# Zeros selected by GpSimd in the exponentials in place of mask products in the second score pass, with the scatters cut into groups around it

## The chip, the cores and the metric

The kernel runs on one core of a Trainium2 chip. The metric is the device time of one execution in microseconds; the lower, the better. Engines are named as the profile does: PE is TensorE (PEld its weight loads), DVE is VectorE, ACT is ScalarE, POOL is GpSimd, SP is SyncE.

## The reference

Sixteen sequences of 512 tokens with 256 features go through layer norm, causal attention with 16 heads of 16, and a mixture of 32 experts of which each token takes four, beside a shared expert:

```python
scores = jnp.einsum('bqhd,bkhd->bhqk', q, k) * scale
causal = jnp.triu(jnp.ones((S, S), dtype=bool), k=1)
scores = jnp.where(causal, -jnp.inf, scores)
attn = jax.nn.softmax(scores, axis=-1)
out = jnp.einsum('bhqk,bkhd->bqhd', attn, v)
...
x = x + _L0_attn_ref(xn, ...) + _L0_ffn_ref(xn, ...)
```

What matters here is the causal mask: a key later than the query must have weight zero.

## The kernel before

The program has three stretches. Phase A goes through the 16 sequences ("batches" below), one after another: attention, the shared expert, and the routing of each token to its four experts. Phase B and C take the 288 blocks of routed tokens through their experts, phase D adds up. Each phase is a block of its own: the next begins when all engines have come to the end of the one before.

In phase A all engines run one list of steps, `ORDER`, and each engine does what its handler for a step says (`run`). So the list sets the order on every engine. The steps of the next sequence's front part (layer norm, q and k products, value and router products) are mixed into the attention of the current one; the last sequence has no next one, and these steps are left out of its list (`attention_steps`). Batch 0 stands ahead of the loop, batches 1 to 14 are the loop, batch 15 is the `tail`.

The heads are done in four groups g of four heads. For each group:

- `("s1", g, u)`, six units: scores with queries on the partitions, for the row maximum. PE multiplies q by k (L937) and adds the mask by a product of the identity with `mask_qk` (L941); DVE takes the maximum (L729). `negsplit` and `negT` (L741, L951) turn the maxima into two extra rows of q, which a DMA puts in place (L409).
- `("s2", g, u)`, five units: scores with keys on the partitions, now less the maximum (L968). PE then adds `mask_kq`, -1e30 above the diagonal, by products with the identity (L979), two a unit. Units 0 and 1 have one diagonal square of 128 columns per head pair, units 2 to 4 have two. ACT writes the exponential of the unit to `probs[g % 2]` (L598). `probs[0]` lies in the space of `we_d`, by which name the trace shows it; `probs[1]` is `probs`.
- `("av", g, kt)`, four steps: the exponentials times the values (L996), kt being the tile of 128 keys. Before, the first of them waits for all five units of the group.

s1 and s2 units share two PSUM buffers (`ps_u`) in turn, so a unit can start when the unit two before it has been read by DVE or ACT.

POOL has two kinds of work in phase A. For `("qk", j)`, j from 0 to 3, it adds the two rope products of DVE (L479), waits until ACT has made the first part (`part0`, L544), and subtracts (L483). For `("scat", t)` it issues for each of the 16 pairs of token tile and expert choice two indirect DMAs, one to `table` (L492) and one to `values` (L494). ACT's `copy` step and DVE's `rankC` of the next batch wait until all of a batch's scatters have landed. In the last batch a step `fill` follows the last scatter: 32 indirect DMAs of zeros (L500). POOL waits for all of them at the end of phase A.

Of the kernel before, what the change touches and what calls it, by code (L numbers as in the profile page):

```python
# [26 lines left out]
BF16 = mybir.dt.bfloat16  # L27
# [7 lines left out]
P = 128  # L35
# [18 lines left out]
REGION = TOKENS  # L54
NBLOCK = TOKENS * TOPK // P + E
TABLE = E * REGION + P
N_CONSTS, N_EARLY, N_IDENT = 24, 22, 4
SKIP = 1 << 24
EPS = 1e-5
MAGIC = float(0x5F3759DF)  # L60
# [8 lines left out]
def hold(eng, passed):  # L69
# [7 lines left out]

ORDER = [
    ("rankC",), ("gate", 0), ("placeV",), ("s1", 0, 0), ("gth", 0), ("up", 0), ("s1", 0, 1), ("copy",), ("s1", 0, 2),
    ("gate", 1), ("s1", 0, 3), ("s1", 0, 4), ("gth", 1), ("scat", 0), ("up", 1), ("lnA",), ("gate", 2), ("s1", 0, 5),  # L80
    ("negsplit", 0), ("gth", 2), ("scat", 1), ("s1", 1, 0), ("up", 2), ("s1", 1, 1), ("negT", 0), ("gate", 3),
# [11 lines left out]
    ("exps",), ("stack", 1), ("down", 0), ("down", 1), ("rankA",), ("av", 3, 0), ("av", 3, 1), ("av", 3, 2),  # L93
    ("av", 3, 3), ("rankB",), ("down", 2), ("avT", 3), ("down", 3), ("aT", 0), ("aT", 1), ("oproj", 0), ("oproj", 1),
]

# [5 lines left out]
def last_steps(order):  # L102


    s, piece = [], 0
    for step in order:
        s.append(step)
        if step == ("rankC",):
            s.append(("fill_rows",))
        if step == ("scat", NT - 1):  # L110
            s.append(("fill",))
        if step[0] == "s2" and step[1:] != (0, 0) and piece < GU_PIECES:
            s.append(("load_gu", piece))
            piece += 1
        if step == ("s2", NG - 1, NU2 - 1):
            s += [("load_d", k) for k in range(D_PIECES)]
    assert piece == GU_PIECES
    return s
# [75 lines left out]
def phase_a(nc, sb_, sem, ident, identb, iota_e, counts, we_gu, we_d, ps_g, ps_u, ps_av, x, wqkvr, wgu_e, wd_e, wo, wgu_s, wd_s, bias,  # L194
            rope_cos, rope_sin, values, sum_dram, table):
    stack = ExitStack()
    with stack:
# [28 lines left out]
        sin_t = in_gu([P, SEQ])  # L226
        ident_r = sb("ident_r", [P, P], F32R)
        mask_qk = sb("mask_qk", [P, P], BF16)
        mask_kq = sb("mask_kq", [P, P], BF16)
        before = sb("before", [P, P], BF16)  # L230
        ones = sb("ones", [P, P], BF16)
        tri_f = sb("tri_f", [P, P])
# [70 lines left out]
        xn_ready, parts_ready, v_placed = sem("xn_ready"), sem("parts_ready"), sem("v_placed")  # L303
        v_ready = sem("v_ready")
        summed, part0_ready = sem("summed"), sem("part0_ready")
        passed_pool, passed_dve, passed_sp = sem("passed_pool"), sem("passed_dve"), sem("passed_sp")
        we_in, fill_chain, fill_ready, filled = sem("we_in"), sem("fill_chain"), sem("fill_ready"), sem("filled")
        neg_parts, tanh_done, av_out, exps, chosen_ready = \
# [119 lines left out]
        def _(pool):  # L428
# [33 lines left out]
                            allow_small_or_imprecise_dtypes=True))  # L462
            zeros_kept(NEG, 0, 1, -1)
            const(pool.tensor_copy(mask_qk[:], tri_f[:]))
            zeros_kept(NEG, 0, -1, 1)
            const(pool.tensor_copy(mask_kq[:], tri_f[:]))
            zeros_kept(1.0, 0, 1, -1)
            const(pool.tensor_copy(before[:], tri_f[:]))
            assert made[0] == N_EARLY
# [14 lines left out]
                                   ALU.subtract).then_inc(parts_ready, 1)  # L484

            def scatter(b, step, env):
                t = step[1]
                pool.wait_ge(xs_ready, NT * b + NT)
                pool.wait_ge(slots, b + 1)
                hold(pool, passed_pool)  # L490
                for k in range(TOPK * t, TOPK * (t + 1)):
                    pool.indirect_dma_start(table[:, :], bass.IndirectOffsetOnAxis(ap=slot[:, k:k + 1], axis=0),  # L492
                                            entry[:, k, :], None).then_inc(scattered, 16)
                    pool.indirect_dma_start(values[:, :], bass.IndirectOffsetOnAxis(ap=slot[:, k:k + 1], axis=0),  # L494
                                            xs[:, k // TOPK, :], None).then_inc(scattered, 16)

            def fill(b, step, env):
                pool.wait_ge(fill_ready, 1)
# [10 lines left out]

                    pool.wait_ge(table_set, 16)  # L510

            run(pool, {"loaded": loaded, "qk": qkv, "scat": scatter, "fill": fill})
            pool.wait_ge(filled, 16 * E)
            pool.wait_ge(scattered, SCATTERS * BATCH)

# [347 lines left out]
        def _(pe_):  # L863
# [92 lines left out]
            def s2(b, step, env):  # L956

                _, g, u = step
                ps = unit_of(step, env)
                if isinstance(b, int) and (b, g, u) == (0, 0, 0):  # L960
                    pe_.wait_ge(consts, N_CONSTS)
                if u == 0:
                    pe_.wait_ge(neg_rows[g % 2], 32 * (2 * b + g // 2 + 1))
                for lo, kt, k in S2_PIECES[u]:
                    n, h = SEQ - kt * P, 2 * g + k
                    for a in range(2):
                        rows = slice(HALF * a, HALF * a + MROWS)
                        nc.tensor.matmul(ps[:, a, lo:lo + n], k_st[rows, h, kt * P:(kt + 1) * P],  # L968
                                         q_st[rows, h, kt * P:SEQ], start=(lo == 0), stop=False, skip_group_check=True)
                for a in range(2):  # L970
                    if u < 2:
                        dst, rhs = ps[:, a, 0:P], mask_kq[:]
                    else:
                        if u < 4:
                            dst = ps[:, a, :].rearrange("p (k n) -> p k n", n=P)[:, 0:NT:3, :]
                        else:
                            dst = ps[:, a, :].rearrange("p (k n) -> p k n", n=2 * P)[:, :, 0:P]
                        rhs = mask_kq[:].rearrange("p (o n) -> p o n", o=1).broadcast_to([P, 2, P])
                    ins = nc.tensor.matmul(dst, identb[:], rhs, start=False, stop=True, skip_group_check=True)  # L979
                ins.then_inc(pe["s2"], 1)  # L980

            def av_(b, step, env):

                _, g, kt = step
                if kt == 0:
                    pe_.wait_ge(S["probs"], done("probs", b, NU2 * g + NU2 - 1))
                    pe_.wait_ge(av_out, NG * b + g)
                    if g == 0:
                        pe_.wait_ge(v_placed, b + 1)
# [489 lines left out]
```

## Time and profile before

| | before |
|---|---|
| median of 3 runs | 2126.34 us (2124.21 to 2130.44) |
| profiled execution, its own time | 2123.62 us |
| its span | 2121.8 us |
| granted PE clock, mean | 0.93 |
| PE busy | 1841.0 us, 87% |
| DVE busy | 1313.1 us, 62% |
| POOL busy | 995.3 us, 47% |
| ACT busy | 812.4 us, 38% |

Phase A takes the first 1475 us or so, phases B and C run to about 2095, phase D takes the rest. A busy share is one over all of the span; what bounds phase A is read from the rows further down.

### The profile page before, as it was taken

To read this page: it belongs to the slowest core of one execution; us is meant where nothing else is said; L and a number is where in the kernel's file an instruction comes from. 1 tells how busy PE (TensorE), PEld (TensorE's weight loads), DVE (VectorE), ACT (ScalarE), POOL (GpSimd) and SP (SyncE) were. 2 spreads that over 40 slices of the span, in tenths; PEclk is the share of its full clock that TensorE was granted. 3 is DMA by queue.
4 is the path that set the end of the run, shared out by engine and by line. 5 is a ranking of instruction groups with operands and counts; after the bars stand their busy time and mean duration, and the time that the engine had idled before them with its cause. 6 is when DMAs were issued, how large, how long until landed. Compare 5 with 4: busy or idle time off the path is not lost. (4 is left out here: it accounts for less than half of the span.)

```text
span 2121.8 us, 42143 instructions
## 1 busy us (share of the span) xinstructions
PE 1841.0 (87%) x10799; PEld 1131.5 (53%) x10800; DVE 1313.1 (62%) x3315; ACT 812.4 (38%) x1763; POOL 995.3 (47%) x993
## 2 busy tenths in 40 slices
PE   5899999999999999999999999996899999999400
PEld 2354554545545455454554545543688888888300
DVE  6656648576585665856648566551566666666487
ACT  2334344353443434435344353432344444445200
POOL 4455344453444534545444453465455565555200
PEclk8999999999999999999999999987899999999755
DMA  6251541615416154161441615466465555555399
GB/s 134 77 123 35 104 79 52 119 37 104 76 55 118 35 106 79 52 122 38 100 80 51 120 37 102 71 169 229 131 176 170 169 175 171 169 165 175 129 351 324
DMA packets 217708, 255.02 MB, mean 120 GB/s; under 512 B 74421, under 2 KB 166334, under 8 KB 217536
## 3 DMA queue, kind: packets, MB, share of 16 engines
q1 hardware_dynamic: 160000, 161.90, 34.2%
q0 software_dynamic: 35840, 71.63, 10.5%
q10 hardware_dynamic: 21824, 20.98, 3.1%
q8 instruction: 19, 0.31, 0.1%
q14 instruction: 25, 0.20, 0.0%
HBM read 112.54 MB, written 94.64 MB: 98 GB/s over the span
## 5 line engine op out<-in xcount | busy, mean ns | idle before, releaser
L729 DVE TENSOR_REDUCE neg<-ps_u 128x2 f32<-128x768 f32 (+3 forms) x384 | 391.6, 1044 | 161.6 <-PE ps_u L941 157.4
L492 POOL DMA_INDIRECT table<-entry,slot x256 | 248.9, 972 | 390.2 <-ACT xs L576 291.7
L1228 POOL DMA_INDIRECT y_dram<-yb,ent x288 | 283.0, 983 | 225.1 <-issue 168.2
L494 POOL DMA_INDIRECT values<-xs,slot x256 | 252.3, 985 | 83.4 <-issue 83.4
L921 PE MATMUL ps_g<-we_gu 128*128 128x512 f32 x512 | 243.7, 609 | 0.0
L937 PE MATMUL ps_u<-k_st,q_st 48*128 48x128 f32 (+3 forms) x1024 | 184.2, 397 | 31.4 <-DVE neg L729 20.3
L598 ACT ACTIVATE probs<-ps_u 128x1024 f32<-128x1024 f32 x160 | 159.6, 1023 | 128.2 <-PE ps_u L979 128.1
L598 ACT ACTIVATE we_d<-ps_u 128x1024 f32<-128x1024 f32 x160 | 160.6, 1022 | 116.9 <-PE ps_u L979 116.9
L968 PE MATMUL ps_u<-q_st,k_st 50*128 50x512 f32 (+3 forms) x1024 | 170.9, 393 | 39.0 <-DMA q_st<-neg_t 16.6
L479 POOL TENSOR_TENSOR we_d<-we_d 128x512 f32<-128x512 f32 x64 | 81.1, 1268 | 216.7 <-DVE we_d L699 216.7
L937 PEld LDWEIGHTS ps_u<-k_st,q_st 48*128 48x128 f32 x1024 | 87.3, 187 | 166.3 <-issue 76.0
L1279 PE MATMUL ps_u<-we_d,h_t 128*128 x576 | 173.8, 384 | 0.0
L1265 PE MATMUL ps_g<-we_gu,x_t 128*128 x576 | 150.8, 385 | 4.4 <-issue 4.4
L968 PEld LDWEIGHTS ps_u<-q_st,k_st 50*128 50x128 f32 x1024 | 88.3, 199 | 122.4 <-ACT probs L598 32.4
L1360 DVE TENSOR_SCALAR wh<-ent 128x1 f32<-128x1 f32 x288 | 44.4, 154 | 176.4 <-ACT tnh L1175 137.5
L1265 PE MATMUL ps_av<-we_gu,x_t 128*128 x576 | 150.1, 383 | 1.6 <-issue 1.5
L1026 PE MATMUL ps_u<-w_d,hid 128*128 128x256 f32 x512 | 135.4, 418 | 0.6
L921 PEld LDWEIGHTS ps_g<-we_gu 128*128 128x128 f32 x512 | 92.8, 194 | 80.2 <-issue 75.5
L1353 DVE COPY x_t<-ps_g 128x256 f32<-128x256 f32 x288 | 120.5, 418 | 12.1 <-PE ps_g L1254 10.5
L941 PE MATMUL ps_u<-mask_qk,identb 128*128 128x128 bf16 (+1 forms) x768 | 125.0, 245 | 0.0
L1189 ACT ACTIVATE yb<-ps_u 128x256 f32<-128x256 f32 x288 | 110.6, 384 | 31.3 <-PE ps_u L1279 5.2
L902 PE MATMUL ps_g<-we_gu 128*128 128x512 f32 x256 | 121.2, 596 | 0.0
(161 smaller groups left out, 3005.4 us busy)
## 6 DMA issues: line engine op xcount, KB each, us to landing
xg<-values SPq DMA_DIRECT2D x288, 128.0 KB
ys<-y_dram SPq DMA_DIRECT2D x64, 512.0 KB, 5.4
q_st<-we_gu SPq DMA_DIRECT2D x192, 128.0 KB, 8.6
k_st<-we_gu SPq DMA_DIRECT2D x192, 128.0 KB, 10.4
we_gu<-x SPq DMA_DIRECT2D x16, 512.0 KB, 5.2
xres<-x SPq DMA_DIRECT2D x16, 512.0 KB, 4.5
sum_dram<-osum SPq DMA_DIRECT2D x16, 512.0 KB, 3.7
we_gu<-wgu_e ACTq DMA_DIRECT2D x16, 512.0 KB, 5.1
```

Of the source, the lines that this page charges most:

```text
L492: pool.indirect_dma_start(table[:, :], bass.IndirectOffsetOnAxis(ap=slot[:, k:k + 1], axis=0), entry[:, k, :], None).then_inc(scattered, 16)
L494: pool.indirect_dma_start(values[:, :], bass.IndirectOffsetOnAxis(ap=slot[:, k:k + 1], axis=0), xs[:, k // TOPK, :], None).then_inc(scatte ...
L598: nc.scalar.activation(probs[g % 2][:, u, :], ps_u[env[1][step][0]][:, :, :].rearrange("p a n -> p (a n)"), ACT.Exp, scale=SCALE).then_inc ...
L729: nc.vector.tensor_reduce(neg[:, g % 2, i, :, k0:k0 + nk], ps[:, :, 0:nk * n].rearrange("p a (k n) -> p a k n", n=n), AX.X, ALU.max, negat ...
L921: ins = nc.tensor.matmul(ps[:, :], w_gu[:, c, lo:lo + P], xn_t[:, c, :], start=(c == 0), stop=(c == KC - 1))
L937: nc.tensor.matmul(ps[:, a, k * n:(k + 1) * n], q_st[rows, h, i * P:(i + 1) * P], k_st[rows, h, 0:n], start=(k == 0), stop=False, skip_gro ...
L941: ins = nc.tensor.matmul(dst, identb[:], mask_qk[:].rearrange("p (o n) -> p o n", o=1).broadcast_to([P, nk, P]), start=False, stop=True, s ...
L968: nc.tensor.matmul(ps[:, a, lo:lo + n], k_st[rows, h, kt * P:(kt + 1) * P], q_st[rows, h, kt * P:SEQ], start=(lo == 0), stop=False, skip_g ...
L1026: nc.tensor.matmul(ps[:, t // 2, (t % 2) * D:(t % 2 + 1) * D], hid[:, m, t * P:(t + 1) * P], w_d[:, m, :], start=(t % 2 == 0 and m == 0), ...
L1228: pool.indirect_dma_start(y_dram[:, :], bass.IndirectOffsetOnAxis(ap=ent[k][:, 0:1], axis=0), yb[k][:, :], None, bounds_check=TOKENS * TOP ...
L1265: ins = nc.tensor.matmul(ps_gu[s][:, 0:2 * HE], x_t[s][:, c * P:(c + 1) * P], w_gu[:, bass.ds(e, 1), c, :], start=(c == 0), stop=(c == KC ...
L1279: nc.tensor.matmul(ps_y[s][:, 0:D], h_t[s][:], w_d[:, bass.ds(e, 1), :], start=True, stop=True).then_inc(y_ps, 1)
```

## The change

`mask_kq` and the 40 products a batch that add it are gone; each score product of s2 is now a group by itself (`start=True, stop=True`). A new step `("zero", g, i)` lets POOL write zeros above the diagonal into the exponentials, in place: i = 0 after units 0 and 1 (one instruction of 4 squares), i = 1 after units 2 and 3 (two instructions), i = 2 after unit 4 (one). Each handles 512 columns on 128 partitions. The first three `av` steps of a group wait for one `zero` step each, the first no longer for all exponentials. `("scat", t)` becomes `("scat", first, end)` in pairs: 8, 2, 2, 1, 1 and 2 of them, at other places in the list, the last two pairs behind `("zero", 3, 2)`. `fill` stays behind the last scatter.

```diff
@@ ORDER (cut)
-    ("gate", 1), ("s1", 0, 3), ("s1", 0, 4), ("gth", 1), ("scat", 0), ("up", 1), ("lnA",), ("gate", 2), ("s1", 0, 5),
+    ("gate", 1), ("s1", 0, 3), ("s1", 0, 4), ("gth", 1), ("scat", 0, 8), ("up", 1), ("lnA",), ("gate", 2), ("s1", 0, 5),
...
@@ last_steps
-        if step == ("scat", NT - 1):
+        if step[0] == "scat" and step[2] == NT * TOPK:
             s.append(("fill",))
@@ gpsimd
+            def zero(b, step, env):
+
+                _, g, i = step
+                u0, nu, step_, cnt = [(0, 2, SEQ, 1), (2, 2, 3 * P, 2), (4, 1, 2 * P, 2)][i]
+                pool.wait_ge(S["probs"], done("probs", b, NU2 * g + u0 + nu - 1))
+                hold(pool, passed_pool)
+                at = probs[g % 2][:, u0:u0 + nu, :].rearrange("p u n -> p (u n)")
+                if cnt == 2 and step_ == 2 * P:
+                    views = [at.rearrange("p (w n) -> p w n", n=2 * P)[:, :, 0:P]]
+                else:
+                    views = [at.rearrange("p (w n) -> p w n", n=SEQ)[:, :, lo:lo + P] for lo in range(0, SEQ, 3 * P)[:cnt]]
+                for view in views:
+                    ins = pool.affine_select(out=view, in_=view, compare_op=ALU.is_ge, fill=0.0, base=0,
+                                             pattern=[[0, 4 if nu > 1 or step_ == 2 * P else 2], [1, P]], channel_multiplier=-1)
+                ins.then_inc(zeroed, 1)
@@ tensor, s2
-                        nc.tensor.matmul(ps[:, a, lo:lo + n], k_st[rows, h, kt * P:(kt + 1) * P],
-                                         q_st[rows, h, kt * P:SEQ], start=(lo == 0), stop=False, skip_group_check=True)
...
-                    ins = nc.tensor.matmul(dst, identb[:], rhs, start=False, stop=True, skip_group_check=True)
+                        ins = nc.tensor.matmul(ps[:, a, lo:lo + n], k_st[rows, h, kt * P:(kt + 1) * P],
+                                               q_st[rows, h, kt * P:SEQ], start=True, stop=True, skip_group_check=True)
@@ tensor, av
+                if kt < 3:
+                    pe_.wait_ge(zeroed, 3 * (NG * b + g) + kt + 1)
                 if kt == 0:
-                    pe_.wait_ge(S["probs"], done("probs", b, NU2 * g + NU2 - 1))
                     pe_.wait_ge(av_out, NG * b + g)
```

Two places on POOL and one on PE show what the list now does. First POOL in the loop, from the subtract of `("qk", 1)` on, around `("qk", 2)`, `("qk", 3)` and group 1 of the heads. Before:

```order
L479 TENSOR_TENSOR we_d<-we_d 128x512 [waits rope,parts_ready]
L483 TENSOR_TENSOR we_gu<-we_d,we_gu 128x512 [waits part0_ready,stacked1]
L475 REGISTER_ALU
L479 TENSOR_TENSOR we_d<-we_d 128x512 [waits rope,parts_ready]
L483 TENSOR_TENSOR we_gu<-we_d,we_gu 128x512 [waits part0_ready,stacked1]
L492 DMA table<-entry,slot 262272x2 [waits xs_ready,slots]
```

The same place in the changed kernel:

```order
L478 TENSOR_TENSOR we_d<-we_d 128x512 [waits rope,parts_ready]
L482 TENSOR_TENSOR we_gu<-we_d,we_gu 128x512 [waits part0_ready,stacked1]
L499 REGISTER_ALU
L507 AFFINE_SELECT probs1<-probs1 128x4x128 [waits probs]
L499 REGISTER_ALU
L507 AFFINE_SELECT probs1<-probs1 128x4x128 [waits probs]
L507 AFFINE_SELECT probs1<-probs1 128x4x128
L474 REGISTER_ALU
L478 TENSOR_TENSOR we_d<-we_d 128x512 [waits rope,parts_ready]
L482 TENSOR_TENSOR we_gu<-we_d,we_gu 128x512 [waits part0_ready,stacked1]
L499 REGISTER_ALU
L507 AFFINE_SELECT probs1<-probs1 128x4x128 [waits probs]
```

Three selects now stand between the subtract of `("qk", 2)` and the add of `("qk", 3)`, and the fourth, `("zero", 1, 2)`, stands behind the subtract of `("qk", 3)`.

PE at `("av", 1, 0)` to `("av", 1, 3)`, in the changed kernel:

```order
L1001 MATMUL ps_av<-probs1,v_pad 32x512 [waits av_out,zeroed]
L1001 MATMUL ps_av<-probs1,v_pad 32x512 x3
L990 REGISTER_ALU
L1001 MATMUL ps_av<-probs1,v_pad 32x384 [waits zeroed]
L1001 MATMUL ps_av<-probs1,v_pad 32x384 x3
L990 REGISTER_ALU
L1001 MATMUL ps_av<-probs1,v_pad 32x256 [waits zeroed]
L1001 MATMUL ps_av<-probs1,v_pad 32x256 x3
L1001 MATMUL ps_av<-probs1,v_pad 32x128 x4
```

Before, only the first of these rows had a wait (`av_out,probs`); now the third key tile waits for the select that stands behind `("qk", 3)` on POOL.

Last, POOL at the end of the last batch, in the changed kernel, from `("zero", 3, 0)` to the end of phase A:

```order
L507 AFFINE_SELECT probs1<-probs1 128x4x128 [waits probs] x2
L507 AFFINE_SELECT probs1<-probs1 128x4x128
L507 AFFINE_SELECT probs1<-probs1 128x4x128 [waits probs]
L490 DMA table<-entry,slot 262272x2 [waits xs_ready,slots]
L492 DMA values<-xs,slot 262144x256
L490 DMA table<-entry,slot 262272x2
L492 DMA values<-xs,slot 262144x256
L514 DMA values<-zeros,fill_row 262144x256 [waits fill_ready]
L514 DMA values<-zeros,fill_row 262144x256 x31
L198 UNCONDITIONAL_BRANCH [waits scattered,filled]
```

Before, the 32 scatters of the batch and the 32 fills followed each other with no wait for `probs` among them; now the last four scatters and all 32 fills stand behind the last exponential of the last batch.

## Rows read from the trace of the kernel before

**Rows 1.** Busy time of each engine in a stretch of one batch (--windows)
```profile
core 0: us, PE busy (x) PEld busy (x) DVE busy (x) ACT busy (x) POOL busy (x), PEclk, DMA share, GB/s
853.90:942.50 88.60, 83.67 (x512) 45.83 (x512) 56.68 (x122) 35.30 (x57) 41.22 (x41) 0.96 0.40 79
```

**Rows 2.** Waits of PE, 300 to 1500 us: total, times, longest
```profile
PE ps_u L968 <- DMA q_st<-neg_t: 14.6, 14, 2.2
PE ps_g L951 <- DVE neg_p L741: 13.3, 14, 1.1
```

**Rows 3.** Timeline of PE, one batch: start us, us, idle before
```profile
714.46 0.28 PE L979 MATMUL ps_u<-mask_kq,identb 128*128 128x128 bf16 x2
714.67 0.50 PE L968 MATMUL ps_u<-q_st,k_st 50*128 50x384 f32 x4
...
715.86 0.50 PE L968 MATMUL ps_u<-q_st,k_st 50*128 50x384 f32 x4 [0.36 <-ACT probs L598]
716.29 0.39 PE L979 MATMUL ps_u<-mask_kq,identb 128*128 128x256 bf16 x2
716.52 1.88 PE L902 MATMUL ps_g<-we_gu 128*128 128x512 f32 x4
...
721.80 2.36 PE L996 MATMUL ps_av<-probs,v_pad 128*32 128x512 f32 x32
724.09 0.44 PE L937 MATMUL ps_u<-k_st,q_st 48*128 48x384 f32 x2
```

**Rows 4.** Timeline of ACT in the same batch
```profile
714.78 2.96 ACT L598 ACTIVATE probs<-ps_u 128x1024 f32<-128x1024 f32 x3 [4.44 <-PE ps_u L979]
717.76 0.63 ACT L544 ACTIVATE we_gu<-we_d 128x512 fp32r<-128x512 f32 x1
...
741.14 4.91 ACT L598 ACTIVATE probs<-ps_u 128x1024 f32<-128x1024 f32 x5 [1.16 <-PE ps_u L979]
```

**Rows 5.** Timeline of POOL in the same batch
```profile
718.54 1.28 POOL L483 TENSOR_TENSOR we_gu<-we_d,we_gu 128x512 fp32r<-128x512 f32 x1 [0.81 <-ACT we_gu L544]
720.77 1.27 POOL L479 TENSOR_TENSOR we_d<-we_d 128x512 f32<-128x512 f32 x1 [0.96 <-DVE we_d L699]
722.85 1.28 POOL L483 TENSOR_TENSOR we_gu<-we_d,we_gu 128x512 fp32r<-128x512 f32 x1 [0.81 <-ACT we_gu L544]
```

**Rows 6.** POOL's groups by form: the selects that there are (mean ns)
```profile
L442 POOL TENSOR_SCALAR_AFFINE_SELECT tri_f<-tri_f 128x128 f32<-128x128 f32 x3 | 0.9, 292 | 0.4
...
L1222 POOL TENSOR_SCALAR_AFFINE_SELECT tri<-tri 32x32 f32<-32x32 f32 x1 | 0.2, 202 | 0.1
```

**Rows 7.** Timeline of POOL at the end of phase A
```profile
1424.60 0.97 POOL L494 DMA_INDIRECT values<-xs,slot  x1 [0.30 <-issue]
1425.87 1.00 POOL L500 DMA_INDIRECT values<-zeros,fill_row  x1 [0.31 <-issue]
...
1465.86 0.98 POOL L500 DMA_INDIRECT values<-zeros,fill_row  x1 [0.30 <-issue]
1478.84 0.37 POOL L1216 IOTA blk_i<- 32x288 f32 x1 [12.00 <-POOLq L197]
```

**Rows 8.** Timeline of ACT at the end of phase A
```profile
1449.38 3.98 ACT L598 ACTIVATE probs<-ps_u 128x1024 f32<-128x1024 f32 x4
```

**Rows 9.** Timeline of SP at the end of phase A
```profile
1468.97 0.40 SPq L415 DMA_DIRECT2D sum_dram<-osum  x1
```

**Rows 10.** Landing times: line L415, and the page's DMA issues (KB, us)
```profile
DMA to landing us min/median/max: 3.1/3.7/5.9
```
```profile
y_dram<-yb,ent POOLq DMA_INDIRECT x288, 2.7
```

**Rows 11.** One step of three batches, timeline of PE
```profile
756.30 0.92 PE L1035 MATMUL ps_u<-w_o,attn_t 128*128 128x256 f32 x3 [0.25 <-ACT attn_t L613]
...
842.55 0.70 PE L1035 MATMUL ps_u<-w_o,attn_t 128*128 128x256 f32 x2 [0.25 <-ACT attn_t L613]
...
931.43 1.35 PE L1035 MATMUL ps_u<-w_o,attn_t 128*128 128x256 f32 x5 [0.25 <-ACT attn_t L613]
```

**Rows 12.** Granted clock (PEclk) of one stretch, columns as in Rows 1
```profile
727.00:735.00 8.00, 7.72 (x36) 4.29 (x34) 2.43 (x5) 3.54 (x5) 6.17 (x7) 0.57 0.19 62
```

More of the change, by code:

```diff
@@ L56 @@
 TABLE = E * REGION + P
-N_CONSTS, N_EARLY, N_IDENT = 24, 22, 4
+N_CONSTS, N_EARLY, N_IDENT = 21, 19, 4
 SKIP = 1 << 24
@@ L79 @@
     ("rankC",), ("gate", 0), ("placeV",), ("s1", 0, 0), ("gth", 0), ("up", 0), ("s1", 0, 1), ("copy",), ("s1", 0, 2),
-    ("gate", 1), ("s1", 0, 3), ("s1", 0, 4), ("gth", 1), ("scat", 0), ("up", 1), ("lnA",), ("gate", 2), ("s1", 0, 5),
-    ("negsplit", 0), ("gth", 2), ("scat", 1), ("s1", 1, 0), ("up", 2), ("s1", 1, 1), ("negT", 0), ("gate", 3),
[11 rows of a table removed]
-    ("exps",), ("stack", 1), ("down", 0), ("down", 1), ("rankA",), ("av", 3, 0), ("av", 3, 1), ("av", 3, 2),
+    ("gate", 1), ("s1", 0, 3), ("s1", 0, 4), ("gth", 1), ("scat", 0, 8), ("up", 1), ("lnA",), ("gate", 2), ("s1", 0, 5),
+    ("negsplit", 0), ("gth", 2), ("s1", 1, 0), ("up", 2), ("s1", 1, 1), ("negT", 0), ("gate", 3),
[6 rows of a table added]
+    ("s2", 1, 4), ("zero", 1, 2), ("negT", 2),
[5 rows of a table added]
+    ("zero", 3, 1), ("rank",), ("s2", 3, 4), ("zero", 3, 2), ("scat", 14, 16), ("exps",), ("stack", 1), ("down", 0), ("down", 1), ("rankA",), ("av", 3, 0), ("av", 3, 1), ("av", 3, 2),
     ("av", 3, 3), ("rankB",), ("down", 2), ("avT", 3), ("down", 3), ("aT", 0), ("aT", 1), ("oproj", 0), ("oproj", 1),
@@ L228, in phase_a @@
         mask_qk = sb("mask_qk", [P, P], BF16)
-        mask_kq = sb("mask_kq", [P, P], BF16)
         before = sb("before", [P, P], BF16)
@@ L305, in phase_a @@
         summed, part0_ready = sem("summed"), sem("part0_ready")
+        zeroed = sem("zeroed")
         passed_pool, passed_dve, passed_sp = sem("passed_pool"), sem("passed_dve"), sem("passed_sp")
@@ L464, in _ @@
             const(pool.tensor_copy(mask_qk[:], tri_f[:]))
-            zeros_kept(NEG, 0, -1, 1)
-            const(pool.tensor_copy(mask_kq[:], tri_f[:]))
             zeros_kept(1.0, 0, 1, -1)
@@ L486, in scatter @@
             def scatter(b, step, env):
-                t = step[1]
                 pool.wait_ge(xs_ready, NT * b + NT)
@@ L490, in scatter @@
                 hold(pool, passed_pool)
-                for k in range(TOPK * t, TOPK * (t + 1)):
+                for k in range(step[1], step[2]):
                     pool.indirect_dma_start(table[:, :], bass.IndirectOffsetOnAxis(ap=slot[:, k:k + 1], axis=0),
@@ L510, in loaded @@
                     pool.wait_ge(table_set, 16)
-            run(pool, {"loaded": loaded, "qk": qkv, "scat": scatter, "fill": fill})
+            run(pool, {"loaded": loaded, "qk": qkv, "scat": scatter, "zero": zero, "fill": fill})
             pool.wait_ge(filled, 16 * E)
@@ L967, in s2 @@
                         rows = slice(HALF * a, HALF * a + MROWS)
-                        nc.tensor.matmul(ps[:, a, lo:lo + n], k_st[rows, h, kt * P:(kt + 1) * P],
-                                         q_st[rows, h, kt * P:SEQ], start=(lo == 0), stop=False, skip_group_check=True)
[L970 to L978, printed above, removed]
-                    ins = nc.tensor.matmul(dst, identb[:], rhs, start=False, stop=True, skip_group_check=True)
+                        ins = nc.tensor.matmul(ps[:, a, lo:lo + n], k_st[rows, h, kt * P:(kt + 1) * P],
+                                               q_st[rows, h, kt * P:SEQ], start=True, stop=True, skip_group_check=True)
                 ins.then_inc(pe["s2"], 1)
```

20 rows, old and new, of the table ORDER are left out of this document.

## The prediction

> **What bounds the kernel now.** I read first the busy time of each engine in a stretch of one batch. In 88.6 us PE is busy 83.67, DVE 56.68, POOL 41.22 and ACT 35.30 [rows 1]. So PE sets the pace of phase A, and what shortens its queue shortens the batch, unless something else is then late. Next I read PE's waits. They are short and belong to chains: over thirteen batches 14.6 us for the DMA of the maxima and 13.3 us for the DVE step ahead of `negT` [rows 2]. The reader is to see that work removed just ahead of such a wait only lengthens the wait. Third comes the timeline of one batch on PE, ACT and POOL, since the change adds a wait of PE on POOL, and POOL works in the order of the list. Last comes the end of phase A, where POOL's last DMAs are issued until 1466.84 [rows 7] and SP's last store is issued at 1468.97 [rows 9]: two ends that lie close together, so either can become the later one.
>
> **What the removal gives.** A pair of mask products takes 714.67 - 714.46 = 0.21 us of PE's time with one square and 716.52 - 716.29 = 0.23 us with two [rows 3]. (Their listed durations, 0.28 and 0.39, overlap the work behind them; the distance to the next start is what goes away.) A batch has 8 of the first and 12 of the second, 4.4 us. Not all of it comes back. ACT needs some 0.99 us for a unit (2.96 for three, 4.91 for five [rows 4]), and PE may be only two units ahead, so in a run of s2 units only the first unit's mask moves the chain of exponentials. By group:
> - group 0: units 0, 3, 4 count, 1 and 2 don't: 0.21 + 0.23 + 0.23 = 0.67.
> - group 1: unit 2 doesn't (the unit behind it waits 0.36 for ACT already [rows 3]): 0.21 + 0.21 + 0.23 + 0.23 = 0.88.
> - group 2: unit 0 is ahead of an s1 unit that waits for DVE, unit 4 ahead of `negT` that waits for DVE [rows 2]; units 1, 2, 3 count. Units 2 and 3 fall in a stretch whose granted clock is 0.57 in the mean [rows 12], so mostly at 1.2 GHz and not 2.4, and count double: 0.21 + 0.46 + 0.46 = 1.13.
> - group 3: five exponentials in one run [rows 4]: only the first mask and the last, 0.44.
>
> Together 3.12 us a batch.
>
> **What a select costs.** The trace has selects of 128 columns (292 ns) and of 32 columns (202 ns) [rows 6]. That is 0.94 ns a column, and 292 + 384 x 0.94 = 653 ns for 512 columns. The bounds: no less than the 292 ns of a select of a quarter of the size, and no more than the 1.27 us of the POOL instruction with two inputs of 512 columns [rows 5]. I take 0.65, because the same operation is in the trace and only its length differs. Sixteen a batch are 10.4 us, and POOL goes from 41.2 to about 52 of 88.6 us busy. It doesn't become the bound; the question is where its work lies.
>
> The page "GPSIMD Engine Reference" of the Trainium skill speaks against the move: its table in section 4.1 gives elementwise work to VectorE, and section 3.1 has 769 ns as measured for 512 elements with one input. By that figure, as an estimate, the four selects in the chain of the next part would take 4 x 0.12 = 0.5 us more a batch, and the sum would be 7 us higher.
>
> **What the order costs PE.** In group 1, POOL's subtract of `("qk", 2)` ends at 718.54 + 1.28 = 719.82 [rows 5]. It follows ACT's part0, which follows the third exponential of the run [rows 4], and this run starts 0.2 earlier now: 719.6. Then come `("zero", 1, 0)` with one select and `("zero", 1, 1)` with two; with 0.1 us ahead of the first they take from 719.7 to 721.7. The add of `("qk", 3)`, before at 720.77 [rows 5], starts at 721.75 and ends at 723.0; ACT's part lies between add and subtract as before (0.81 us of idle [rows 5]); the subtract ends at 725.1, and `("zero", 1, 2)` at 725.9. PE can go on with the third key tile at 726.0.
>
> Where would PE be? Before, av(1) runs from 721.80 to 724.09 [rows 3]. Less the masks of units 1, 3 and 4 of this group it starts at about 721.15; the four key tiles have 512, 384, 256 and 128 columns, so the third starts at 70% of the 2.29 us, at 722.75. PE stands idle for 726.0 - 722.75 = 3.25 us, in each of the 15 batches that have qk steps. Behind it in PE's queue are the s1 and s2 units of groups 3 and 2, and so DVE and ACT wait too: nothing makes up for it. The bounds by the price of a select (four of them lie in this chain): 3.25 - 4 x 0.36 = 1.8 us and 3.25 + 4 x 0.62 = 5.7 us.
>
> At the other av steps I find no wait. In group 0 the 16 scatters are done before the exponentials matter; in group 2 the select behind one scatter pair (2.5 us) ends about when the third key tile comes, and PE waits for a DMA right behind it anyway [rows 2]; in group 3 the down products lie between. The last scatters of a batch stand behind the last exponentials now; what hides them is the end of the batch on PE (av, down and output products) ahead of the next `rankC`, and if they landed behind that, DVE and then PE would wait there.
>
> Per batch: 3.25 - 3.12 = +0.13 us, over 15 batches +2 us. The whole gain on PE goes into the wait.
>
> **What the order costs at the end of phase A.** In the last batch POOL ran from scatter to fill with no wait; the fills took 1465.86 - 1425.87 = 39.99 us for 31 starts, 1.29 each, and the last ended at 1466.84 [rows 7]. Now four scatters and 32 fills stand behind `("zero", 3, 2)`, and that behind the last exponential, which ended at 1449.38 + 3.98 = 1453.36 [rows 8]. The masks ahead of it in this batch give at most 2.9; more of its units queue on ACT and DVE, and I take 2.3: 1451.1. Then 0.1 + 0.65 for the select, 4 x 1.27 = 5.1 for the scatters (spacing 1425.87 - 1424.60 [rows 7]), 32 x 1.29 = 41.3 for the fills: the last ends at 1498.2. Landing: 2.7 us from issue as the scatters of phase B have it [rows 10], so 1499.9. Before, the last store was issued at 1468.97 [rows 9] and lands 3.7 later [rows 10], at 1472.7; POOL's first instruction of phase B came at 1478.84 [rows 7], 6.1 later. Now it comes at 1506.0: +27.2 us. Nothing covers it, since phase B starts behind the barrier.
>
> **Sum.** 2 + 27.2 = +29 us, from a span of 2121.8 to about 2151. The profiled execution's own time is 2123.62, 1.8 over its span and 2.7 under the median of the runs; against the median 2126.34 I forecast **2155.5 us**, 1.4% slower. About 0.3% (6 us) is what a measurement of this kernel can tell from no change.
>
> **Rivals.**
> - *More time at the low clock.* Most batches have one stretch at 1.2 GHz such as [rows 12]. The batch that ends at 842.55 has none and took 86.25, the one after took 88.88 [rows 11]: one stretch costs 2.6 us. The clock falls in group 2, after a few waits of 0.3 to 0.4 us. Now a wait of 3 us comes just ahead, and the dense products of the masks are gone. If a second stretch follows in each batch: 15 x 2.6 = +39, 2195 us. Against it: the fall may only come where it comes already. Chance 0.22. The page "TensorE: Matmul & The Clock Gate", Part 1, says that the throttled state is the default and activity releases it; that would speak for this rival, and by it alone I would raise its chance.
> - *A select costs as much as a two-input instruction*, 1.27 us: the wait is 5.7, so +37 more, 2192 us. For it: 3-dimensional views with strides, which the rows do not show. Chance 0.11.
> - *av(1) is not late* (the other side): POOL's selects would fit ahead of PE. Then the 3.12 us come back in full: -47 + 27 = -20, 2107 us, faster. It decides from the point where the wait at the third key tile is under 3.12 - 27.2 / 15 = 1.3 us; that is below my lower bound of 1.8. For it: POOL's listed spans are rough, and a PE that keeps more of the 4.4 us moves the point. Chance 0.14.
> - *The low stretch goes away* because the order of waits changes: at most in 14 of the 15 batches, -36, with the two costs as forecast: 2119 us, at the edge of 0.3%. Chance 0.08.
> - *The mask gain is whole*, 4.4 us and not 3.1, with the rest as forecast: -19, 2136 us. Part of the range of the forecast.
>
> **How the numbers follow.** Forecast 0.45; its own range is 2136 (the mask gain whole) to 2174 (a select of 0.96 us, half way to its upper bound: 15 x 4 x 0.31 = +19). The others 0.22, 0.11, 0.14, 0.08. The range leaves out the fast rival and a little above: 2118 to 2198. Faster: 0.14 and 0.03 of the last rival but one, 0.17. Same: the rest of that rival's 0.08 and a little of the forecast's lower edge, 0.08. Slower: 0.75.
>
> **What would show it.** The rows of the mask products are gone and s2 units lie 0.2 us closer. A select of 128x4x128 shows 0.65 us. PE's waits have a new row, av on POOL, about 3 us in 15 batches, in one step of group 1. POOL's fills run from about 1459 to 1500 and phase B starts some 27 us later. Wrong would be: no such wait (POOL in time), a select of over 1 us, a batch with two stretches of low clock, or PE waiting for `rankC` because the late scatters land late.

## The result, and the profile after

The changed kernel takes 2213.02 us in the median (2207.28 to 2217.81, 4 runs) against 2125.28 us before: a ratio of 1.042, 95% interval 1.0383 to 1.0457. It is 88 us slower, three times the 29 us that I forecast, and above the range. The span grew from 2121.8 to 2211.8 us, the mean granted clock fell from 0.930 to 0.886.

The waits of PE in the changed kernel, over the whole span: who waited for whom, us in total, times, longest:

```profile
PE ps_av L1001 <- POOL probs L507: 40.0, 15, 3.0
PE ps_u L982 <- ACT probs L612: 24.4, 49, 0.9
PE ps_g L965 <- DVE neg_p L755: 23.6, 31, 1.4
```

The first row is new, and it is the wait that was forecast: 15 times, 2.67 us each (forecast 3.25). (L507 is the select, L982 the s2 product, L965 `negT`.) The two below it are larger than before (ACT `probs` 5.9, `neg_p` 16.5 us over phase A): PE's units are shorter by their masks, the ACT and DVE steps that they wait for are not.

Where the wait sits is read from the timelines of one batch. PE:

```profile
1116.38 0.74 PE L982 MATMUL ps_u<-q_st,k_st 50*128 50x512 f32 x6
1118.01 0.50 PE L982 MATMUL ps_u<-q_st,k_st 50*128 50x384 f32 x4 [0.88 <-ACT probs L612]
...
1123.60 1.71 PE L1001 MATMUL ps_av<-probs,v_pad 128*32 128x512 f32 x16
1127.91 0.86 PE L1001 MATMUL ps_av<-probs,v_pad 128*32 128x256 f32 x16 [2.60 <-POOL probs L507]
```

and POOL in the same batch:

```profile
1120.91 1.27 POOL L482 TENSOR_TENSOR we_gu<-we_d,we_gu 128x512 fp32r<-128x512 f32 x1 [0.81 <-ACT we_gu L558]
1122.13 1.81 POOL L507 TENSOR_SCALAR_AFFINE_SELECT probs<-probs 128x512 f32<-128x512 f32 x3
1123.91 1.28 POOL L478 TENSOR_TENSOR we_d<-we_d 128x512 f32<-128x512 f32 x1
1126.00 1.26 POOL L482 TENSOR_TENSOR we_gu<-we_d,we_gu 128x512 fp32r<-128x512 f32 x1 [0.81 <-ACT we_gu L558]
1127.22 0.64 POOL L507 TENSOR_SCALAR_AFFINE_SELECT probs<-probs 128x512 f32<-128x512 f32 x1
```

This is the queue of the prediction: subtract, three selects, add, 0.81 us for ACT, subtract, and only then the select for which the third key tile waits. The wait at L982 has gone from 0.36 us [rows 3] to 0.88: a mask taken out in the middle of a run of exponentials.

What I had left to a rival is in the granted clock. The columns are those of [rows 1]; the first fence is the middle of phase A before, the second the same stretch after, with the two stretches that follow the wait shown above:

```profile
600.00:1300.00 700.00, 659.64 (x4067) 359.03 (x4067) 448.05 (x961) 283.95 (x447) 327.33 (x316) 0.97 0.40 78
```
```profile
600.00:1300.00 700.00, 633.67 (x3581) 336.96 (x3572) 435.10 (x928) 263.69 (x423) 385.94 (x420) 0.91 0.37 76
...
1124.00:1128.00 4.00, 1.40 (x20) 0.35 (x16) 0.93 (x1) 0.63 (x1) 3.04 (x3) 1.00 0.01 2
1129.00:1147.00 18.00, 16.57 (x84) 7.96 (x82) 9.26 (x27) 7.65 (x11) 9.60 (x11) 0.53 0.21 54
1149.00:1154.00 5.00, 4.52 (x23) 3.58 (x22) 1.78 (x8) 2.34 (x4) 3.35 (x6) 0.66 1.09 132
```

The clock is at 2.4 GHz while PE stands, falls to 1.2 GHz within 2 us of PE going on at 1127.91, and stays there for most of 18 us; a short second stretch follows. In windows of 1 us all 15 batches with the wait show this fall right behind it; the stretch is 17 or 18 us long in eight of them and 11 in the other seven. Before, a stretch in the middle batches was 7 or 8 us long [rows 12]. As a measure of the low clock I add up, over phase A until PE's last product, stretch length times one minus the granted clock ("clock loss", worked out from windows of 1 us): 61 us before, 150 us after. It is read from one execution of each kernel; `e4_fill_spread` below, whose batches 0 to 14 are those of the changed kernel, shows 164, so differences of 15 us or less say nothing.

The end of phase A, POOL:

```profile
1515.69 0.98 POOL L490 DMA_INDIRECT table<-entry,slot  x1 [0.16 <-issue]
...
1520.80 1.00 POOL L514 DMA_INDIRECT values<-zeros,fill_row  x1 [0.31 <-issue]
...
1560.83 0.98 POOL L514 DMA_INDIRECT values<-zeros,fill_row  x1 [0.30 <-issue]
1571.27 0.37 POOL L1221 IOTA blk_i<- 32x288 f32 x1 [9.45 <-POOLq L198]
```

and ACT there, whose last exponential ends at 1514.46:

```profile
1513.41 1.05 ACT L612 ACTIVATE probs<-ps_u 128x1024 f32<-128x1024 f32 x1
```

From the end of the last exponential to POOL's first instruction of phase B it is 56.8 us now, 25.5 before (1478.84 - 1453.36, [rows 7, 8]): 31.3 us for the late fill. Phase B begins 92.4 us later; so the late fill has 31 us of it and the batches 61, of which 40 are PE standing for POOL. (Of the 31, 6.3 us are the last select and four scatters, which stand between the exponential and the first fill: 1520.80 - 1514.46.)

### The profile page after: what moved, and what is told of

Read it like the earlier page. It is cut to its first block and busy times, and to the rows that moved or that the text cites. A ratio compares the mean times of both kernels' runs of the same rounds, so it can differ in the third digit from the quotient of the medians.

```text
span 2211.8 us, 41662 instructions
## 1 busy us (share of the span) xinstructions
PE 1833.7 (83%) x10159; PEld 1116.1 (50%) x10160; DVE 1315.4 (59%) x3315; ACT 806.6 (36%) x1763; POOL 1152.3 (52%) x1246
## 5 line engine op out<-in xcount | busy, mean ns | idle before, releaser
L935 PE MATMUL ps_g<-we_gu 128*128 128x512 f32 x512 | 243.3, 608 | 0.0
L951 PE MATMUL ps_u<-k_st,q_st 48*128 48x128 f32 (+3 forms) x1024 | 198.1, 425 | 36.9 <-DVE neg L743 21.4
L982 PE MATMUL ps_u<-q_st,k_st 50*128 50x512 f32 (+3 forms) x1024 | 168.0, 410 | 48.1 <-ACT probs L612 24.4
L612 ACT ACTIVATE probs<-ps_u 128x1024 f32<-128x1024 f32 x160 | 153.5, 1030 | 86.8 <-PE ps_u L982 84.5
L951 PEld LDWEIGHTS ps_u<-k_st,q_st 48*128 48x128 f32 x1024 | 92.9, 198 | 181.6 <-issue 72.7
L982 PEld LDWEIGHTS ps_u<-q_st,k_st 50*128 50x128 f32 x1024 | 93.2, 216 | 130.7 <-ACT probs L612 49.2
L955 PE MATMUL ps_u<-mask_qk,identb 128*128 128x128 bf16 (+1 forms) x768 | 131.0, 256 | 0.0
L916 PE MATMUL ps_g<-we_gu 128*128 128x512 f32 x256 | 127.4, 621 | 0.0
```

The lines of the kernel that those rows point to most:

```text
L612: nc.scalar.activation(probs[g % 2][:, u, :], ps_u[env[1][step][0]][:, :, :].rearrange("p a n -> p (a n)"), ACT.Exp, scale=SCALE).then_inc ...
L935: ins = nc.tensor.matmul(ps[:, :], w_gu[:, c, lo:lo + P], xn_t[:, c, :], start=(c == 0), stop=(c == KC - 1))
L951: nc.tensor.matmul(ps[:, a, k * n:(k + 1) * n], q_st[rows, h, i * P:(i + 1) * P], k_st[rows, h, 0:n], start=(k == 0), stop=False, skip_gro ...
L955: ins = nc.tensor.matmul(dst, identb[:], mask_qk[:].rearrange("p (o n) -> p o n", o=1).broadcast_to([P, nk, P]), start=False, stop=True, s ...
L982: ins = nc.tensor.matmul(ps[:, a, lo:lo + n], k_st[rows, h, kt * P:(kt + 1) * P], q_st[rows, h, kt * P:SEQ], start=True, stop=True, skip_g ...
```

## The experiments

Two theories of the batches' 61 us were put against each other. **Wait theory**: PE's wait for POOL brings the extra low clock. **Thin-work theory**: the clock falls because the dense mask products are gone. Each ratio is to the kernel before on the same chip; differences between two variants that ran on different chips carry the 3 us by which the kernel before differs there (2123.10 to 2126.31).

**Masks out, nothing else** (`e1_no_masks`; nothing above the diagonal is zeroed).

```diff
-  q_st[rows, h, kt * P:SEQ], start=(lo == 0), stop=False, skip_group_check=True)
-  ... # the loop over a that adds mask_kq
+  q_st[rows, h, kt * P:SEQ], start=True, stop=True, skip_group_check=True)
```


> The kernel before with the mask products of s2 taken out and nothing in their place: no selects, scatters and fill where they were, PE waits for the exponentials as before. What lies above the diagonal is not zeroed, so this leaves out half of the causal mask. Wait theory (the extra time at 1.2 GHz in the changed kernel comes from PE's wait for POOL): no such wait here, the clock stays about as before (mean some 0.93) and the time falls by the 3.1 us a batch that I worked out: about 2075 us. Thin-work theory (the clock falls because the dense bf16 products are gone): the stretches at the low clock grow as in the changed kernel, by about 4 us a batch, and the time is 2125 - 50 + 60 = about 2135 us with a mean clock near 0.89.

Measured: 2095.73 us, ratio 0.9865 (0.9834 to 0.9895), 30.6 us faster; clock loss 68 us, not to be told from 61. The clock stays, against the thin-work theory taken alone. But the gain is 1.9 us a batch, not 3.1. PE's waits in one batch give the place:

```profile
858.89 0.50 PE L968 MATMUL ps_u<-q_st,k_st 50*128 50x384 f32 x4 [0.88 <-ACT we_d L598]
859.81 0.44 PE L937 MATMUL ps_u<-k_st,q_st 48*128 48x384 f32 x2 [0.41 <-ACT we_d L598]
...
882.35 0.50 PE L968 MATMUL ps_u<-q_st,k_st 50*128 50x384 f32 x4 [0.88 <-ACT probs L598]
...
899.61 0.59 PE L951 MATMUL ps_g<-ident_r,neg_p 128*8 128x128 f32 x4 [1.60 <-DVE neg_p L741]
...
908.20 3.72 PE L1016 MATMUL ps_u<-w_d,hid 128*128 128x256 f32 x16 [0.41 <-ACT probs L598]
```

Before, the waits there were 0.46, none, 0.36, 1.08 and none. Over that batch all waits of PE sum to 7.2 us against 4.65 in the batch before the change that ends at 842.55: 2.6 of the 4.4 us of masks come back as waits, where I had counted 1.3. The last row is one I had counted as saved: the down products take over a score buffer and wait for ACT's run of five.

**Masks kept, all else changed** (`e2_masks_kept`): the mask products are back on PE beside the selects.

```diff
+  ... # the loop over a that adds mask_kq, as before the change
```


> The changed kernel with the mask products of s2 put back on PE, so that the selects write zeros where there are zeros already. The wait for POOL and the late fill stay. Wait theory: the low clock stays as in the changed kernel and the masks add up to 3.1 us a batch: 2213 + 50 = about 2260 us. Thin-work theory: the low clock goes back to that of before (about 4 us a batch less): 2213 + 50 - 60 = about 2200 us.

Measured: 2200.71 us, ratio 1.0346 (1.0322 to 1.0371); PE waits 31.5 us for POOL, clock loss 92 us. With the masks the kernel is faster than without them: 12 us less, though PE has 640 products more. So a wait with the masks in place costs more than its length (clock loss 61 to 92), and with the masks out it costs more still (150). The two waits are not quite the same: 2.1 us a batch here, 2.67 in the changed kernel. With the masks the clock falls behind the wait in 11 of the 15 batches, without them in all.

**The third and fourth key tile later on PE** (`e3_av_later`); `avT` of the group moves one unit back with them.

```diff
-  ("av", 1, 0), ("av", 1, 1), ("av", 1, 2), ("av", 1, 3), ("scat", 10, 12), ("s1", 3, 2), ("s2", 2, 0), ("s1", 3, 3),
-  ("s1", 3, 4), ("s2", 2, 1), ("zero", 2, 0), ("avT", 1), ("s2", 2, 2),
+  ("av", 1, 0), ("av", 1, 1), ("scat", 10, 12), ("s1", 3, 2), ("s2", 2, 0), ("s1", 3, 3), ("s1", 3, 4),
+  ("av", 1, 2), ("av", 1, 3), ("s2", 2, 1), ("zero", 2, 0), ("s2", 2, 2), ("avT", 1),
```


> The changed kernel with the third and fourth key tile of group 1 four steps later on PE (behind the s1 and s2 units that followed them), so that POOL's select is done when PE comes to them. Masks stay out, the fill stays late. Wait theory: 2.7 us of wait and about 4 us of low clock a batch go away, 15 x 6.7 = 100: about 2113 us, the clock at about 0.93. Thin-work theory: the wait alone goes: 2213 - 40 = about 2173 us, the clock stays near 0.89.

Measured: 2142.26 us, ratio 1.0074 (1.0048 to 1.0101), 71 us off; clock loss 90 us. The wait's 40 us and 30 more go. The measured time lies between the two forecasts.

**The select between POOL's add and subtract**, where POOL waits 0.81 us anyway. PE's order is untouched. It ran twice: first on a chip on which the kernel before took 2641.82 us (told at the end), then on another.

```diff
   pool.tensor_tensor(rq[:, j % 2, :], rp1[:, j % 2, :], rp2[:, j % 2, :], ALU.add).then_inc(summed, 1)
...
+  if j == 3 and not env[3]:
+      zero(env[2], ("zero", 1, 2), env)
   pool.wait_ge(part0_ready, NCH * nb + j + 1)
```


> The changed kernel with the last select of group 1 put between POOL's add and subtract for the q/k step 3, where POOL waits for ACT anyway; PE's order is that of the changed kernel. The wait at the third key tile shrinks from 2.7 to about 0.7 us: 15 x 2 = -30 us from that alone, 2183 us (thin-work theory, clock still near 0.89). Wait theory: nearly all the extra low clock goes too, 60 us more, about 2125 us. If both are needed together (what the masks kept and the later av steps suggest): in between, near the later av steps, 2145 to 2160 us with Sum of low clock near 90 us in phase A.

> The same kernel once more on another chip: the changed kernel with the last select of group 1 between POOL's add and subtract for q/k step 3. Thin-work theory: only the wait shrinks, 2183 us. Wait theory: the wait and nearly all extra low clock, 2125 us. Both needed: 2145 to 2160 us.

Measured on the second chip: 2147.36 us, ratio 1.011 (1.0069 to 1.015). PE's waits in phase A:

```profile
PE ps_u L988 <- ACT probs L618: 24.1, 49, 0.9
...
PE ps_av L1007 <- POOL probs L509: 8.7, 15, 1.0
```

31 us of wait gone, 66 us of time gone, clock loss from 150 to 94 us. It is the cleanest pair: one instruction moved on an engine that is not the bottleneck. Over half of what it saves is clock: PE's busy time in phase A, with the same products, falls from 1320.8 to 1277.2 us (rows further down). Neither theory alone forecasts it (2183 and 2125); "both together" does (2145 to 2160).

**The late fill.** In the kernel before, the fills alone wait for the last exponential:

```diff
   def fill(b, step, env):
+      pool.wait_ge(S["probs"], done("probs", b, NG * NU2 - 1))
       pool.wait_ge(fill_ready, 1)
```


> The kernel before, with one wait added on POOL in the last batch: the 32 fills wait for the last exponential. Nothing else is touched; all scatters are issued before. My account of the end of phase A: fills from about 1453.5 to 1494.8, landing and barrier as forecast: phase B starts some 24 us later, 2126 + 24 = about 2150 us. If the end of phase A is set otherwise: 2126 us, no change.

> The same kernel once more on another chip, since on the first one both kernels took some 500 us more than elsewhere: the kernel before with the 32 fills of the last batch waiting for the last exponential. Late fill as I account for it: +24 us, 2126 to 2150. Otherwise: no change.

Measured on the second chip: 2147.03 us, ratio 1.0113 (1.0074 to 1.0151), +23.3 us; on the first 0.9946 (0.9926 to 0.9966): there the late fill cost nothing that can be seen, against the forecast, and why is not known. POOL in the second chip's trace:

```profile
1451.85 0.99 POOL L501 DMA_INDIRECT values<-zeros,fill_row  x1 [27.26 <-ACT probs L599]
...
1502.26 0.37 POOL L1217 IOTA blk_i<- 32x288 f32 x1 [9.44 <-POOLq L197]
```

Phase B starts 23.4 us later than before, as worked out. The other way round, the fills cut up in the changed kernel (`e4_fill_spread`):

```diff
+FILL_AT = {("scat", 8, 10): (0, 6), ("zero", 1, 0): (6, 7), ("scat", 10, 12): (7, 12), ("zero", 2, 0): (12, 13),
+           ("scat", 13, 14): (13, 16), ("scat", 14, 16): (16, 32)}
```


> The changed kernel with the 32 fills of the last batch in six pieces, 16 of them in POOL's idle time between selects and scatters, 16 behind the last scatter. My account of the end of phase A (+27 us forecast for the late fill, +31 by the two traces): 16 x 1.29 = 20.6 us come off, 2192 us. If instead the end of phase A is set by something else (the weight loads or the last output product), it stays within 5 us of 2213.

Measured: 2199.57 us, ratio 1.035 (1.0328 to 1.0372), 13.4 us off instead of 20.6. In the traces the end of phase A is shorter by the full amount and more: from PE's last product to phase B it is 20.2 us instead of 42.7. But PE's last product ends 9 us later. Some 6 us of this were there before the last batch, in batches that the edit does not touch (its clock loss is 164 against 150). In the last batch the fills in POOL's "idle" time made a select late, and PE with it:

```profile
1513.99 1.51 PE L1003 MATMUL ps_av<-we_d,v_pad 128*32 128x256 f32 x16 [1.58 <-POOL we_d L509]
```

**The selects on a scratch tile** (`e8`, `f8`): POOL waits for the exponentials and selects as in the change, but on other data and with a wait of 0.17 us between one select and the next, and PE waits for the exponentials alone. Nothing above the diagonal is zeroed; the last batch has POOL's waits but no selects.

```diff
+  view = aside[:, 0, :].rearrange("p (w n) -> p w n", n=P)
...
-  pe_.wait_ge(zeroed, 3 * (NG * b + g) + kt + 1)
+  pe_.wait_ge(S["probs"], done("probs", b, NU2 * g + NU2 - 1))
```


> The changed kernel with the selects of batches 0 to 14 working on a scratch tile instead of the exponentials (those of the last batch are left out, its waits on POOL stay), and PE waiting for the exponentials as before. So nothing above the diagonal is zeroed; masks are out, POOL has its selects, the scatters and the late fill are where the change put them. If POOL's work costs the others nothing: e1 (2096) + late fill (31) = about 2127 us, low clock as in e1. If POOL's selects or the moved scatters slow other engines or make DVE wait: up to 2143 us, as with the later av steps.

> The same kernel once more on another chip: selects on a scratch tile (none in the last batch), PE waits for the exponentials as before, masks out, scatters and late fill as in the change; nothing above the diagonal is zeroed. POOL's work costs the others nothing: 2127 us. It slows them or lowers the clock: up to 2143 us.

Measured on the second chip: 2161.79 us, ratio 1.0188 (1.0151 to 1.0224); clock loss 107 us. This was a miss: no wait of PE for POOL, and still 35 us over what masks out and late fill give. DVE's timeline shows a wait that the kernel before does not have, of `rankC` for the last scatters of the batch before, which are issued behind the last selects now:

```profile
1117.60 0.69 DVE L787 TENSOR_TENSOR osum<-ps_u,xres 128x512 f32<-128x512 f32 x1 [0.85 <-PE ps_u L1049]
1120.29 0.18 DVE L846 TENSOR_TENSOR entry<-pr,zs 128x16 f32<-128x16 f32 x1 [1.99 <-DMA values<-xs,slot]
```

The last of those scatters is issued at 1109.12 and landed only at about 1120. These waits sum to 12.4 us here, and to none in the kernel before. In the changed kernel they are 1.3 us, in `e4_fill_spread` with the same batches 9.1; the cover that I had named and not priced is thin indeed.

**The last two scatter pairs ahead of the selects of group 3**, the fill staying behind the last select step, `("zero", 3, 2)`: once with the selects aside, once with the select between add and subtract.

```diff
-  ("zero", 2, 2), ("scat", 13, 14), ...  ("zero", 3, 2), ("scat", 14, 16), ("exps",)
+  ("zero", 2, 2), ("scat", 13, 16), ...  ("zero", 3, 2), ("exps",)
```


> The variant with selects on a scratch tile (nothing above the diagonal zeroed, none in the last batch, PE waits for the exponentials alone), with the last two scatter pairs before the selects of group 3 and the fill still behind the last exponential. If the late scatters made DVE wait (12.4 us in all) and the clock fall (about 30 us): 2162 - 42 = about 2120 us, which is the masks alone (2096) and the late fill (23). If the selects themselves or the waits on POOL are what lowers the clock: about 2150 us.

> The variant with the last select of group 1 between add and subtract, with the last two scatter pairs before the selects of group 3 and the fill still behind the last select. If late scatters cost as above: from 2147 down by the 3.2 us of DVE's wait and part of the low clock, 2130 to 2140 us. If not: 2147 us.

Measured: with selects aside 2116.35 us (nine runs from 2106.75 to 2133.10, and one of 3169.37 that nothing here explains), ratio 0.997 (0.9942 to 0.9998), clock loss 72 us and no wait of DVE left. So from `f8` 45 us went, 12 of them wait; PE's busy time in phase A falls from 1289.9 to 1261.2 us, which is that of masks out alone (1260.4). With the scatters early, then, POOL's 240 selects cost the others nothing: PE's last product ends at 1438.4 us, in `e1_no_masks` at 1441.6. With the select between: 2146.06 us, ratio 1.0104 (1.0078 to 1.013), no change where 2130 to 2140 was forecast, clock loss 95. There the DVE wait was only 3.2 us to begin with, and the 8.7 us of PE's wait for POOL remained.

**Versions meant to be faster.** Masks by products and no selects in group 1 and in the whole last batch:

```diff
+def masks_in(b, g):
+    return g == 1 or (isinstance(b, int) and b == BATCH - 1)
```


> A version meant to be faster: the changed kernel with mask products kept (and no selects) in group 1 of every batch and in the whole last batch. Then POOL has no select around the q/k step 3, PE has no wait for it, and the fill has no exponential ahead of it. By the removal alone the masks gave 30 us in 16 batches of four groups; three groups in 15 batches are 0.70 of it: 2126 - 21 = about 2105 us, low clock near that of before. If thinner work lowers the clock with whatever small wait is left: 2115 to 2125 us.

> The same kernel once more on another chip: masks by products and no selects in group 1 of each batch and in the whole last batch, the rest as changed. Masks alone: 2105 us. If thinner work and small waits lower the clock: 2115 to 2125 us.

Measured on the second chip: 2112.55 us, ratio 0.9946 (0.9928 to 0.9964), 0.5% under the kernel before and below both kernels; clock loss 63 us, no wait of PE for POOL. It lies between the two forecasts. With the scatters early as well (`h2`), and with group 3's masks kept too (`h1`):

```diff
-    return g == 1 or (isinstance(b, int) and b == BATCH - 1)
+    return g in (1, 3) or (isinstance(b, int) and b == BATCH - 1)
```


> The variant with masks kept in group 1 and in the last batch, with the last two scatter pairs of a batch issued before the selects of group 3. The landing wait of DVE (3.8 us in all) and perhaps some low clock behind it go away: 2104 to 2110 us. If the landing of the scatters costs nothing: 2112 us, no change.

> Masks by products in groups 1 and 3 and in the whole last batch, selects in groups 0 and 2 alone; the last three scatter pairs of a batch go out together before group 3. Group 3 gave only 0.4 us a batch by my count, and no DVE wait for late scatters is left: as fast as the variant with masks kept in group 1 or up to 5 us faster, 2108 to 2113 us. If the gain comes from all groups alike: 2116 us.

Measured: `h2` 2110.52 us, ratio 0.9932 (0.9914 to 0.9951), not told apart from the one before it; `h1` 2117.99 us, ratio 0.9973 (0.9959 to 0.9988). The two differ in group 3's masks alone: taking them out is worth some 7 us, where I had counted 0.44 us a batch.

## Why the prediction was wrong

The direction and both places were right; the size was not. By its own steps:

- **What the removal gives**, forecast 3.12 us a batch, 47 to 50 us. Measured alone: 30.6. The count of the units that wait for nothing was wrong: more of them stand ahead of a wait for ACT or DVE than I found, the last unit of group 3 among them, which I had as saved and behind which the down products now wait 0.41 us.
- **What a select costs**, forecast 0.65 us. Measured 0.637 (median of 256). The strided views cost nothing extra. Where the Trainium skill has 769 ns for 512 elements with one input ("GPSIMD Engine Reference", section 3.1), this operation was faster.
- **What the order costs PE**, forecast 3.25 us in 15 batches. Measured 2.67: 40 us for 49.
- **What the order costs at the end of phase A**, forecast +27.2. Measured alone 23.3, in the changed kernel 31.3 by the traces.
- **Sum.** These steps with their measured sizes give -31 + 40 + 31 = +40 us, against a forecast of 29. That they lie so near is in part luck: the gain was put about 17 us too high and the wait 9 too high, with opposite signs. What is missing are the other 48 of the 88 us.
- **The step that failed** is "Per batch: 3.25 - 3.12 = +0.13 us": it has no term for the clock. I had named one among the rivals, a second stretch at the low clock in each batch, 15 x 2.6 = +39 us, with chance 0.22, and held against it that the fall may only come where it comes already. It came behind the new wait in all 15 batches, for 11 to 18 us, and PE's same products take 60.4 us longer than with the masks out alone (rows below). The rival was right in its cause and too small in its size: 2195 us against 2213.

What the clock costs can be read without the measure of clock loss, from PE's busy time in phase A. The rows are, in this order, the kernel before and masks kept; then masks out alone, the select between, and the changed kernel. The columns are those of [rows 1]:

```profile
52.00:1473.00 1421.00, 1327.12 (x8110) 717.59 (x8110) 882.92 (x1880) 560.49 (x872) 685.28 (x664) 0.96 0.41 89
52.00:1550.00 1498.00, 1355.56 (x8110) 718.41 (x8108) 887.01 (x1880) 560.97 (x872) 839.61 (x920) 0.93 0.39 84
```
```profile
52.00:1448.00 1396.00, 1260.36 (x7476) 671.35 (x7474) 885.11 (x1880) 553.48 (x873) 680.73 (x664) 0.95 0.42 90
52.00:1496.00 1444.00, 1277.24 (x7466) 676.50 (x7464) 884.52 (x1879) 553.74 (x872) 840.26 (x920) 0.92 0.40 87
52.00:1565.00 1513.00, 1320.80 (x7467) 701.80 (x7465) 884.80 (x1879) 554.77 (x872) 842.57 (x920) 0.89 0.38 83
```

Within each fence PE does the same products. With the masks in, the wait and the rest of the change make them 28.4 us longer; with the masks out, 60.4 us, of which 43.6 go when one select is moved. The start of phase B adds up from this: masks out alone 25.0 us earlier (1453.82 against 1478.84), 60.4 for the longer products, 26.6 for more idle time of PE (40 for POOL, less 13 of other waits), 30.5 for the end of the phase, together the 92.4 us that it moved.

What was shown is this. PE's wait for POOL brings more low clock: the fall stands right behind it, and either remedy for the wait takes off most of the extra. Masks out alone does not (68 against 61). Wait and masks out together give more (150) than the wait with the masks in (92), so neither theory by itself holds. Why they give more is not shown: PE's work behind the gap is thinner, but the gap is also longer (2.67 against 2.1 us), and no run holds it equal. In `f8` some low clock went away with the late scatters; that DVE's wait brought it is likely, not shown, for behind the wait shown, which ends at 1120.29, the clock falls only at 1142. "TensorE: Matmul & The Clock Gate", Part 1, of the Trainium skill says that activity releases the throttle; the runs agree in direction, since the granted clock is 0.53 behind the wait of 2.6 us. Why one marginal stretch falls and a like one does not stays open: in `e1` PE has waits of 0.88 and 0.41 us at 858.89 and of 0.89 and 0.41 at 944.26, and the clock falls behind the second alone.

## What to carry to other kernels

Before work is moved off the bottleneck engine, walk the queue of the engine that takes it: it is not its busy share (52 of 88.6 us) that counts but what stands ahead of the one instruction that is waited for. A wait on TensorE is to be priced with its clock: here 31 us less wait in 15 batches gave back 66 us. It can pay to leave part of the work where it was: with 30% of the mask products kept, so that neither the wait nor the late fill arose, the kernel was 0.5% faster than before, and with all of them moved 4% slower. Where a batch loop is tuned, look at the last iteration by itself: a chain of 32 DMAs that had been free became 23 to 31 us when one step came ahead of it.

## What the runs showed of the hardware that was not expected

- On one chip the kernel before took 2641.82 us (13 runs, 2635.88 to 2652.29), elsewhere 2123 to 2126. The trace of the late fill taken there shows ACT and DVE in single waits of up to 15.7 and 12.1 us, put down to nothing on the core (ACT `neg_t` 115.9 us, DVE `neg` 109.9 us between 600 and 1500 us), while POOL goes on issuing its scatters. There the versions with fewer mask products were much faster than before (0.9227, 0.9163 and 0.928 for select between, selects aside and masks kept in group 1), the late fill not slower. I didn't find what makes that difference; no conclusion here rests on that chip.
- The last scatters of 128 rows in `f8`, issued while the stacking DMAs keep the DMA engines full (share 1.09 from 1109 to 1120), take about 10 us to land, by the end of DVE's wait for them; in phase B indirect DMAs land in 2.7 us [rows 10] at a share of 0.61.
- More products on TensorE made a kernel faster: masks kept against masks out, 2200.71 and 2213.02 us, ratios to before of 1.0346 and 1.042 whose intervals (to 1.0371, from 1.0383) don't meet. PE's busy time in phase A is longer with the masks all the same, 1355.6 against 1320.8 us; it is its idle time that is shorter.
